# Between two layers: the last two token tiles normed and routed one at a time, and the routing steps placed sooner among the output products

## What is computed

```
x = layernorm(x + latent_attention(x))   # 16 heads, rotary part, causal softmax, output product Wo
x = layernorm(x + experts(x))            # sigmoid router, top 2 of 16 experts, gate/up, silu, down
x = layernorm(x + grouped_attention(x))  # 16 query heads, 4 key heads, alibi, tanh cap
x = layernorm(x + x @ binarised(W).T + bias)
```

```
logits = x @ gate_w.T ; p = sigmoid(logits)      # 1024 tokens x 16 experts
w, idx = top_k(p, 2)                              # two experts a token
```

## Time and profile before

| what | value |
|---|---|
| median of three runs | 531.9 us (531.44 to 535.48) |
| the profiled execution | 533.71 us, of which its span is 531.9 us |
| mean granted clock of PE in it | 0.975 |
| PE, DVE, ACT, POOL busy | 93%, 71%, 66%, 59% of the span |
| last output product of the first attention ends | 204.2 us |
| first block of the expert loop transposed from | 221.2 us |

### The profile page before, as it was taken

How to read it: one execution, slowest core, us unless ns; L and a number is a source line. 1 busy time by engine, 2 the same in 40 slices (tenths; PEclk the granted TensorE clock), 3 DMA queues, 4 the chain that set the end, 5 groups by cost and what they waited for, 6 DMA issues and landing times.

```text
span 531.9 us, 10859 instructions
## 1 busy us (share of the span) xinstructions
PE 495.0 (93%) x3648; PEld 435.9 (82%) x3648; DVE 377.6 (71%) x833; ACT 350.2 (66%) x791; POOL 315.7 (59%) x319
## 2 busy tenths in 40 slices
PE   8999999999999996899957979999999999999994
PEld 6768888888888785688846869999999999999884
DVE  3798888878874275655547897779757986578656
ACT  4768788877877656334423776778766876686673
POOL 5749898889885136255550676677544664465330
PEclk9999999999999999799987998999999999999998
DMA  8929999940000582345565000000000000000001
GB/s 261 394 73 362 321 340 321 327 171 2 0 2 1 169 351 82 111 141 163 170 236 178 2 0 1 1 1 3 1 0 1 1 2 2 1 0 1 2 22 59
DMA packets 17761, 56.84 MB, mean 107 GB/s; under 512 B 2628, under 2 KB 12362, under 8 KB 15914
## 3 DMA queue, kind: packets, MB, share of 16 engines
q1 hardware_dynamic: 14960, 49.81, 27.6%
q0 software_dynamic: 2752, 6.40, 3.6%
HBM read 49.19 MB, written 28.45 MB: 146 GB/s over the span
## 4 chain that ended last, share of the span: by engine, by line
PE 64%; DVE 9%; POOL 8%; issue 8%; ACT 8%; DMA 3%; POOLq 0%; SPq 0%; ACTq 0%; DVEq 0%
PE bank L450 10%; PE bank L452 10%; PE bank L451 10%; PE bank L1007 5%; PE bank L515 5%; POOL qT L2021 3%; ACT probs L1138 2%; PE bank L751 2%; PE bank L736 2%; PE bank L738 2%; PE bank L737 2%; PE bank L1024 2%; PE bank L718 2%; POOL probs L2029 2%; PE bank L627 2%
## 5 line engine op out<-in xcount | busy, mean ns | idle before, releaser
L1138 ACT ACTIVATE probs<-bank,neg_max,q_scale 128x256 f32<-128x256 f32 (+1 forms) x128 | 63.8, 509 | 22.6 <-DVE neg_max L1813 22.6
L2071 POOL TENSOR_TENSOR exps<-exps,tables 128x256 f32<-128x256 f32 x32 | 24.7, 770 | 75.2 <-ACT exps L1253 75.1
L2029 POOL TENSOR_TENSOR probs<-probs,inv_sum 128x512 f32<-128x512 f32 x64 | 51.7, 829 | 21.5 <-DVE inv_sum L1821 21.5
L1253 ACT ACTIVATE exps<-bank 128x768 f32<-128x768 f32 x32 | 25.9, 809 | 41.2 <-PE bank L718 41.2
L1633 DVE TENSOR_TENSOR q_lo<-q_sum,q_hi 128x512 fp32r<-128x512 f32 x32 | 28.6, 893 | 29.1 <-ACT q_hi L1207 28.8
L2167 POOL DMA_INDIRECT y_rows<-y_slot,dest x31 | 29.7, 957 | 30.3 <-issue 19.2
L2058 POOL TENSOR_TENSOR swapped<-swapped,tables 128x512 f32<-128x512 f32 x32 | 43.3, 1355 | 5.2 <-ACT swapped L1174 5.1
L1799 DVE TENSOR_TENSOR swapped<-bank,tables 32x512 f32<-32x512 f32 x64 | 44.4, 693 | 1.4
L2021 POOL TENSOR_TENSOR qT<-qT,swapped 128x512 f32<-128x512 f32 x32 | 41.0, 1282 | 6.1 <-DVE swapped L1799 6.1
L450 PE MATMUL bank<-x,wq_hi 128*128 128x256 f32 x128 | 38.6, 301 | 0.1
L450 PE MATMUL bank<-wo_hi,c_hi 128*128 128x256 f32 x128 | 37.5, 293 | 0.0
(11 more groups left out here) (291 smaller groups left out, 1857.4 us busy)
## 6 DMA issues: line engine op xcount, KB each, us to landing
slots<-in_c_unused SPq DMA_DIRECT2D x20, 1036.0 KB, 35.3
gu_all<-in_gate_up SPq DMA_DIRECT2D x4, 1024.0 KB, 8.9
xg<-slots SPq DMA_DIRECT2D x31, 129.5 KB
wvo_raw<-in_wvo SPq DMA_DIRECT2D x1, 2560.0 KB, 19.5
dn_all<-in_down SPq DMA_DIRECT2D x1, 2048.0 KB, 8.0
wq_full<-in_Wq SPq DMA_DIRECT2D x1, 2048.0 KB
wo_raw<-in_Wo SPq DMA_DIRECT2D x1, 2048.0 KB
wqk_raw<-in_wqk SPq DMA_DIRECT2D x1, 1536.0 KB, 11.5
```

The source lines that it names most:

```text
L1138: ins = act.activation(probs[:, par, h, c0:c1], bank[:, 2 * par + h, c0:c1], ACT.Exp, bias=neg_max[:, par, i:i + 1], scale=q_scale[:, b, t ...
L2029: ins = pool.tensor_tensor(some, some, inv, ALU.mult)
```

## The change

Routing goes by five groups in place of four: tiles (0,1), (2,3), (4,5), and then tile 6 and tile 7 each by itself. The square roots of tiles 6 and 7 are taken apart under one load of the Sqrt table, with tile 6's copy between them. In PE's order, transposes now stand ahead of product i = 0 of the odd tile, logits after i = 1, and the prefix after i = 0 of the next even tile; the prefix of group 2 stands ahead of the last product of tile 7. Tile 6 is transposed right behind that last product. The filler products between the last groups are 8 in place of 14 and go to bank 0. On DVE, `place` comes ahead of the norm of the next group for groups 0 and 1, and both weight splits stand behind the norm of group 1. The other edits renumber semaphore counts for the fifth group.

```diff
-WARM = (20, 42, 18, 14)
+WARM = (20, 42, 18, 8)
+    routed_together = [(0, 1), (2, 3), (4, 5), (6,), (7,)]
...
             for i in range(PAIRS):
+                if i == 0 and t >= 3 and t % 2:
+                    pe_transpose_x(eng, b - 1)
                 pe_out0(eng, t, i)
                 if i == 1 and t >= 3 and t % 2:
-                    pe_transpose_x(eng, b - 1)
-                if i == 4 and t >= 3 and t % 2:
                     pe_logits(eng, b - 1)
-                if i == 4 and t >= 4 and t % 2 == 0:
+                    pe_offsets(eng, b - 1)
+                if i == 0 and t >= 4 and t % 2 == 0:
                     pe_prefix(eng, b - 2)
-        pe_prefix(eng, B - 2)
-        keep_busy(eng, WARM[3])
-        pe_transpose_x(eng, B - 1)
-        pe_logits(eng, B - 1)
-        pe_prefix(eng, B - 1)
+                if i == PAIRS - 2 and t == NT - 1:
+                    pe_prefix(eng, 2)
+        pe_transpose_x(eng, 3)
+        pe_logits(eng, 3)
+        pe_offsets(eng, 3)
+        keep_busy(eng, WARM[3], 0)
+        pe_transpose_x(eng, 4)
+        pe_logits(eng, 4)
+        pe_prefix(eng, 3)
+        pe_offsets(eng, 4)
+        pe_prefix(eng, 4)
...
+        for g in range(B):
+            if g >= 1:
+                x_turned(g - 1)
+                act_sigmoid(act, g - 1)
+            load_table(act, 2 * g + 1, ACT.Sqrt)
+            root(g)
+            if g == B - 1:
+                x_turned(g)
+                root(g + 1)
+            load_table(act, 2 * g + 2, ACT.Sigmoid)
...
+        act_sigmoid(act, B - 1)
+        x_turned(B)
+        act_sigmoid(act, B)
...
+        for b in range(B - 1):
+            if b >= 1:
+                pick(b - 1)
...
+            dve_statistics(dve, counted, 0, b)
+            if b >= 1:
+                place(b - 1)
+            normalise(b)
+            if b == 1:
...
+                dve.tensor_tensor(wk_lo[:], wk_raw, raw(wk_hi[:]), ALU.subtract).then_inc(kv["kv_lo"], 1)
                 dve.tensor_tensor(wv_lo[:], wv_raw, raw(wv_hi[:]), ALU.subtract).then_inc(kv["kv_lo"], 1)
...
+        add_y(6)
+        tile_moments(6)
+        pick(2)
+        normalise(3)
+        place(2)
+        add_y(7)
+        tile_moments(7)
+        normalise(4)
+        pick(3)
+        place(3)
+        pick(4)
+        place(4)
...
-            for t in (2 * b, 2 * b + 1):
+        for g, tiles in enumerate(routed_together):
+            pool.wait_ge(mo["slots_ready"], g + 1)
+            for t in tiles:
```

More of the change, by code:

```diff
@@ L504, in keep_busy @@
-    def keep_busy(pe, n):
+            eng.wait_ge(mo["marked"], g)
+            eng.wait_ge(mo["slots_ready"], g)
+        tiles = routed_together[g]
+        eng.matmul(prefix_of(g), ident_bf[:], region_bf[:].unsqueeze(1).broadcast_to([P, len(tiles), E]), start=True,
+                   stop=False, skip_group_check=True)
+        for t in range(tiles[0]):
+            if g == 1 and t == 0:
+                eng.wait_ge(ld["alibi_in"], 48)
+            eng.matmul(prefix_of(g), ones_bf, marks[:, t:t + 1, :].broadcast_to([P, len(tiles), E]), start=False,
+                       stop=False, skip_group_check=True)
@@ new lines, in pe_prefix @@
+    def pe_prefix(eng, g):
+        eng.wait_ge(mo["marked"], g + 1)
+        if g == 0:
+            eng.wait_ge(ld["alibi_in"], 48)
+        tiles = routed_together[g]
+        mm = eng.matmul(prefix_of(g), earlier, marks[:, tiles_of(g), :], start=False, stop=len(tiles) == 1,
+                        skip_group_check=True)
+        if len(tiles) == 2:
+            mm = eng.matmul(prefix_of(g)[:, E:2 * E], ones_bf, marks[:, tiles[0], :], start=False, stop=True,
+                            skip_group_check=True)
+        mm.then_inc(mo["prefix_done"], 1)
@@ L1212, in act_tile_hi @@
     def act_tile_hi(act, norm, b, j):
-        act.wait_ge(ln["xT_done"], done_tile(norm, b, j))
+        act.wait_ge(ln["xT_done"], done_tile(norm, b, j) + 1)
         act.activation(x1[:, b, 0, :, j * P:j * P + P],
@@ L1454, in tile_moments, with normalise @@
             dve.bn_aggr(moments[:, t, :], bn_out[:, t, :]).then_inc(ln["var_ready"], 1)
[L1456 to L1460, removed]
+        def normalise(g):
+            dve.wait_ge(ln["sqrt_done"], root_of(0, g))
+            dve.wait_ge(dve_step, counted(dve.reciprocal(inv_dev[:, 0, tiles_of(g)], deviation[:, 0, tiles_of(g)])))
+            for t in routed_together[g]:
+                dve.tensor_scalar(x_tok[:, t, :], x_tok[:, t, :], moments[:, t, 0:1], inv_dev[:, 0, t:t + 1],
+                                  ALU.subtract, ALU.mult).then_inc(ln["x_new"], 1)
@@ L1909, in step, with each, pick @@
             dve.wait_ge(dve_step, counted(ins))
-        def each(x, n):
-            return x.unsqueeze(1).unsqueeze(1).broadcast_to([P, 2, TOP, n])
-        def pick(b):
-            two, tiles = slice(2 * b, 2 * b + 2), (2 * b, 2 * b + 1)
-            dve.wait_ge(mo["sigmoid_done"], b + 1)
+        def each(x, tiles, n):
+            return x.unsqueeze(1).unsqueeze(1).broadcast_to([P, tiles, TOP, n])
+        def pick(g):
+            some, tiles, n = tiles_of(g), routed_together[g], len(routed_together[g])
+            dve.wait_ge(mo["sigmoid_done"], g + 1)
             for t in tiles:
```

144 lines of the change are left out of this document (58 added, 86 removed).

## The result

The changed kernel takes 535.61 us (median of 20 runs, 534.45 to 537.7), the kernel before 532.26 beside it (20 runs, 530.73 to 535.72): ratio 1.0057, 95% interval 1.0042 to 1.0073. By that ratio it is slower by 3.0 us; forecast was 0.8 faster, within 529.8 to 533.2. Run twice more, on chips 6 and 2, the changed kernel gave 1.0074 (1.0045 to 1.0103) and 1.0077 (1.0035 to 1.012).

What follows compares the result with a forecast made beforehand. The prediction took the block loads to wait for the later of the last scatter's landing and last slot numbers + 6.1; release 0.8 sooner (218.0 for 218.77) made 531.9 - 0.8 = 531.1, range 529.8 to 533.2.

Steps and rivals of the forecast that it cites:

- Tile 7 ... pick to 211.1, prefix to 211.3, place to 211.75: DVE's last routing steps before the block loads: last slot numbers taken at 211.9, kept within 211.6 to 212.6.
- POOL's eight scatters: Last scatters between the layers: in one piece from 205.85, last starting at 214.7 and landed at 217.6, 1.2 sooner.
- block 0 is transposed: PE's start on the expert blocks: expected near 220.5, as a sign that the forecast holds.
- tile 3's logits: PE in the output products: waits 1.15 for ACT's copy, so tile 3 ends at 188.3, not 187.2.
- Group 2's scatters: POOL between the layers: start at 205.85, 0.4 later than 205.48, and end at 210.9 without idling before tile 6's.
- SP's wait for the scatters: SP's queue before the block loads: 0.9 before, expected none or almost none; 0.5 or more would show the forecast wrong.
- bound (b): SP's address reads end 6.1 after the last slot numbers, at 218.0, releasing the block load 0.8 sooner than 218.77.
- PE's filler ends after 221: Sign of being wrong: PE's 42 filler products before block 0 were expected to end near 220.4.
- Rival 3: Slower: tile 7's slots late, 213.5 with hops 0.1 longer and one more stall of 0.6; +0.8, 532.7; chance 0.2.
- price rule: Last slot numbers between the layers: from 212.7 on, the kernel is slower than before, one for one.
- Rival 5: Something outside the stretch between the layers, such as the clock in a later one; either sign, could pass 1%; chance 0.05.
- allowed for this between the layers only: PE's clock during the 42 fillers: if low throughout, they take 9.2 and the gain is 0 to 0.1.

Runs made afterwards that it cites:

- ACT held: Changed kernel with ACT's eight wq_hi copies held until PE's three sums of the counts are done: 0.9979 of before on chip 13, 1.0053 on chip 0.
- set 5: Three runs on chip 2: changed kernel, 1.0077; the same with tile 6's scatters waiting for tile 7's slots, 0.9997; the split alone with that wait, 1.0018.
- tile 6's scatters held: Changed kernel, but POOL starts tile 6's two scatters only when tile 7's slots are there too: 0.9997 of before, on chip 2.
- more fillers: Changed kernel with 6, 8 and 3 filler products added between PE's last small steps: 1.0068 of before, on chip 6.
- set 3: Three runs on chip 13: changed kernel with scatters from group 2 held, 1.0167, or ACT's copies held, 0.9979; kernel before with group 1's scatters held, 1.0106.
- the two of chip 13: Changed kernel with ACT's wq_hi copies held until the counts are done, 0.9979; kernel before with group 1's scatters held until group 2's slots, 1.0106.

## Why the prediction was wrong

**The sum had the wrong sign through one term.** The step that failed is "Tile 7 ... pick to 211.1, prefix to 211.3, place to 211.75": the prefix was priced at 0.2, by the rows of before, and DVE waited 3.1 for it. On the clock of before, tile 7's slots came at 213.28 + 1.95 = 215.2, not 211.9. Of these 3.3, 2.9 is the prefix's late completion; the rest stands ahead of it, mostly tile 6's prefix, 0.4 late, behind which DVE picks tile 7 (marks at 209.69 + 1.95 = 211.6 for 211.1). All that hangs behind the slots moved one for one.

**What the sum was right in.** Where no product is late (ACT held, first chip), the last slots come at 33.46 from the common start, that is 212.0 on the clock of before (forecast 211.9), POOL's eight scatters have no gap, and block 0 is transposed 0.4 sooner than before (220.8; forecast 220.5). The time was 0.9979 of before, -1.1 us with an interval from -2.6 to +0.4, where -0.8 was forecast; the interval takes in both and no change. The step was sized as it runs undisturbed. That this run had nothing late is luck, or the chip.

**Step by step**, in after's trace. PE idles 1.20 ahead of tile 3's logits (forecast 1.15), right. Group 2's scatters start at 204.19 + 1.95 = 206.1 (205.85), and run into tile 6's without a gap, right. SP's wait for the scatters is gone and its address reads are what releases the block load, right: bound (b), last slots + 6.1, gives 215.2 + 6.1 = 221.3, and the last read ends at 219.10 + 0.15 + 1.95 = 221.2. "PE's filler ends after 221" was named as a sign that I would be wrong: it ended at 214.36 + 7.17 + 1.95 = 223.5. One thing was not foreseen and costs nothing here: the first scatter of group 0 takes 3.21 where DVE's two weight splits (1.22 each) run beside it. Group 0's scatters still end at 196.71, ahead of group 1's slots at 197.29.

**The rivals.** Rival 3 said slower, with chance 0.2, and its price rule held: from 212.7 on one for one, 215.2 - 212.7 = 2.5 against 2.58 measured at block 0. Its mechanism did not: it had tile 7's steps late by queueing (hops of 0.1 more, a stall of 0.6), for 0.8 in all. The queues behaved; completions were late, and no row of before shows one: even its products that run beside scatters (set 5) are on time. What I should have said is that the change moves tile 7's prefix and the sum of marks from POOL's idle time into its busiest stretch, and that their 0.2 was read where POOL stood idle. That stood in no rival.

**The clock.** Rival 5 (0.05) came true as an addition of about 1.0: from layer 1's first product to the end, before takes 353.34 - 109.16 = 244.2 and after 356.63 - 111.42 = 245.2. All three traces of the changed kernel start layer 1 at the lower level, 1.2 GHz (0.41 for a product). So does the trace of ACT held on the first chip, whose end is then 0.5 later than before's although its layer 1 begins 0.5 sooner, while that of tile 6's scatters held starts it at 2.4 GHz (0.28 for a product, 244.1 to the end). Over all 20 traces, the ten with the lower level in the first microseconds of layer 1 take 244.9 to 245.6 from there to the end, and the other ten 243.3 to 244.3, but for one (more fillers, 245.3). The Trainium skill (TensorE: Matmul & The Clock Gate, Part 1) has the gate's window free-running, so that the same work meets the turn at another place; the traces agree, in that layer 1 starts at either level. I had allowed for this between the layers only, where it changed nothing: the 42 fillers took 7.17 (7.43 before).

## What to carry to other kernels

Before you fill an engine's idle time, ask what ran undisturbed in it: POOL's pause of 1.83 was the quiet in which PE's prefix completed in 0.2. Durations read from a quiet stretch can be too short once the work is moved beside a stream of scatters: here 0.2 became 3.1. And a wait on "remote" or on an unknown queue on one core deserves the first look, ahead of the long rows. One profile and one chip that confirm a theory are not enough when the thing comes and goes: the same kernel gave 0.998 and 1.005. Run the kernel that has the fault on the same chip as each cure; set 3 didn't, and its three kernels told nothing for sure.

## What the hardware showed that was not expected

- Products of PE (0.2 to 0.4 by the record) whose completion came 0.4 to 5.6 us behind their modelled end, where 0.02 is usual. This is so in twelve of the 15 traces with tiles 6 and 7 apart; the other three are tile 6's scatters held (0.27) and the two of chip 13. It is so in none of the five traces with the two tiles together, whose products run beside scatters too.
- An indirect scatter's issue on POOL of 3.2 beside two DVE operations of 128x1024 elements back to back (1.22 each), in all twelve traces with that order, and 1.13 where one of them is nearly over. In both cases it ends 0.93 behind DVE's last (192.89 and 191.96 after, 192.95 and 192.02 before).
- The same start of layer 1 at 0.28 or 0.41 us for a product, as the clock happened to stand, which goes with about 1.0 us of the total.
